# The row transform of the next image at the end of this image's program

## The reference

```
f      = fftshift(fft2(x))                        per image and channel
amp    = |f|;  gate = sigmoid(amp w_h + b_h) + sigmoid(amp w_l + b_l)
s      = real(ifft2(ifftshift(f * gate)))         the phase is kept
y      = silu(conv3x3(s, w_f) + b_f) + x
z      = layernorm(y) * gamma + beta              over channels

u      = layernorm(z);  y = mamba2(u)             512 rows, each a sequence of 128
z      = z + ff(y);     out = z + fc2(gelu(fc1(layernorm(z))))
```

## Time and profile before

| | |
|---|---|
| median of 3 runs | 4281.23 us (4280.12 to 4282.1) |
| the profiled execution | 4282.0 us, its span 4280.1 us |
| busy, share of the span | PE 93%, DVE 82%, ACT 75%, POOL 60% |
| span of the four images | about 1700 us, some 415 to 440 us each |
| mean granted clock of TensorE | 0.974 of full |

### The profile page before, as it was taken

One profiled execution on the slowest core, in us unless ns is written; L12 is line 12 of the kernel. 1 busy time (PEld: TensorE's weight loads), 2 busy tenths in 40 slices (PEclk: granted clock), 3 DMA queues, 4 the chain that ended last, 5 costly groups with the idle time before them and its releaser, 6 DMA issues.

```text
span 4280.1 us, 95150 instructions
## 1 busy us (share of the span) xinstructions
PE 3983.8 (93%) x31687; PEld 2863.5 (67%) x31687; DVE 3492.5 (82%) x8772; ACT 3194.4 (75%) x4968; POOL 2587.1 (60%) x2713
## 2 busy tenths in 40 slices
PE   7998898799979985799999999999999999999998
PEld 4787578757865885466666666666666666666665
DVE  4568447745775485699999999999999999999997
ACT  4445534553456354699999999999999999999997
POOL 0036103600460056588888888888888888888886
PEclk9999999999989998899999999999999999999999
DMA  2013101400140022111111111111111111111110
GB/s 91 1 53 129 57 2 63 156 20 11 63 164 3 11 72 81 38 41 38 42 39 42 39 42 39 42 39 42 39 39 40 39 42 39 42 39 42 39 42 26
DMA packets 214865, 205.93 MB, mean 48 GB/s; under 512 B 14368, under 2 KB 149152, under 8 KB 214688
## 3 DMA queue, kind: packets, MB, share of 16 engines
q1 hardware_dynamic: 214688, 203.60, 14.6%
HBM read 136.45 MB, written 67.11 MB: 48 GB/s over the span
## 4 chain that ended last, share of the span: by engine, by line
PE 58%; ACT 0%; DVE 0%; POOL 0%; issue 0%; POOLq 0%; DVEq 0%; ACTq 0%
PE g_ps L1043 7%; PE g_ps L1028 6%; PE g_ps L986 6%; PE g_ps L972 5%; PE g_ps L1031 5%; PE g_ps L1060 5%; PE g_ps L1003 3%; PE g_ps L1073 3%; PE g_ps L1079 3%; PE g_ps L1052 3%; PE g_ps L1012 3%; PE g_ps L977 3%; PE g_ps L992 2%; PE g_ps L1068 2%; PE g_ps L965 2%; PE g_ps L997 1%
## 5 line engine op out<-in xcount | busy, mean ns | idle before, releaser
L1355 DVE TENSOR_TENSOR g_mmat<-g_emat,g_ps 128x1024 f32<-128x1024 f32 x512 | 598.9, 1210 | 1.4 <-PE g_ps L1003 1.4
L1194 ACT ACTIVATE g_emat<-g_ps 128x1024 f32<-128x1024 f32 x512 | 521.1, 1024 | 85.7 <-PE g_ps L1031 84.2
L1298 DVE SCALAR_TENSOR_TENSOR g_acc<-g_ps,g_conv_w,g_acc 128x504 f32<-128x504 f32 (+1 forms) x768 | 554.5, 722 | 10.3 <-ACT g_acc L1157 9.9
L873 POOL TENSOR_TENSOR g_acc<-g_acc,g_tap 128x508 f32<-128x508 f32 x384 | 482.5, 1271 | 123.6 <-DVE g_acc L1298 123.6
L613 POOL MEMSET f_s_hi<- 128x192 f32 x4 | 1.0, 258 | 820.7 <-PE f_ps L344 820.7
L1043 PEld LDWEIGHTS g_ps<-g_mmat,g_dtx 128*32 128x32 f32 x8192 | 192.6, 109 | 310.6 <-issue 181.7
L1028 PE MATMUL g_ps<-g_rz,g_l 128*128 128x512 f32 x1024 | 390.0, 462 | 1.6 <-DVE g_z L1383 1.6
L229 PE MATMUL f_ps<-f_s_hi,f_wf_hi 128*128 128x256 f32 x1152 | 360.3, 313 | 5.0 <-DVE f_s_lo L466 5.0
L415 ACT ACTIVATE f_s_hi<-f_ps 128x384 fp32r<-128x384 f32 x256 | 125.7, 491 | 274.0 <-PE f_ps L217 268.9
L1043 PE MATMUL g_ps<-g_mmat,g_dtx 128*32 128x128 f32 x8192 | 329.2, 279 | 0.0
L230 PE MATMUL f_ps<-f_s_lo,f_wf_hi 128*128 128x256 f32 x1152 | 326.2, 283 | 0.0
(11 more groups left out here) (194 smaller groups left out, 12374.3 us busy)
## 6 DMA issues: line engine op xcount, KB each, us to landing
f_xt<-in_x_cols SPq DMA_DIRECT2D x32, 1024.0 KB, 10.3
f_xres<-in_x SPq DMA_DIRECT2D x128, 256.0 KB, 2.8
z<-f_zout SPq DMA_DIRECT2D x128, 256.0 KB, 2.0
g_zin<-z SPq DMA_DIRECT2D x128, 256.0 KB, 2.7
g_zres<-z SPq DMA_DIRECT2D x128, 256.0 KB, 2.9
out<-g_outb SPq DMA_DIRECT2D x128, 256.0 KB, 3.0
f_wf_raw<-in_w_f SPq DMA_DIRECT2D x1, 576.0 KB, 6.9
g_wx<-in_in_proj_t SPq DMA_DIRECT2D x1, 192.0 KB, 2.3
```

The costliest lines, as they stand in the source:

```text
L873: pool.tensor_tensor(acc[:, j, :, 1:], acc[:, j, :, 1:], tap1[:, j, :, 0:P - 1], ALU.add).then_inc(add_p[j], 1)
L1194: act.activation(emat[:, g, :].rearrange("p (b n) -> p b n", b=2), ps[:, D_BANK[g]:D_BANK[g] + 2, :], ACT.Exp).then_inc(e_a[g], 1)
L1298: dve.scalar_tensor_tensor(out=acc[:, j, :, k:], in0=four(ps[:, bank, :])[:, :, 0:P - k], scalar=conv_w[:, j, 3 - k:4 - k], in1=acc[:, j, ...
L1355: dve.tensor_tensor(mmat[:, g, :].rearrange("p (h n) -> p h n", h=HEADS), emat[:, g, :].rearrange("p (h n) -> p h n", h=HEADS), ps[:, CB, ...
```

## The change

The row transform of image b + 1 becomes the last part of image b's program on PE; that of image 0 stands ahead of the loop. The loop over images runs three times, and the last image is written out after it. On ACT and DVE the loop over the eight tiles becomes `row_copy(b, t)`, written out, and its calls for the next image stand among the last steps of this image's convolution:

- ACT: copies 0 and 1 after `center(13, .)`, then `center(14, 0)`, copy 2, `center(14, 1)`, copy 3, `center(15, 0)`, copy 4, `center(15, 1)`, copies 5, 6 and 7.
- DVE: `residual(15, 0)`, `residual(15, 1)`, copy 0, `moments(15, 0)`, copy 1, `moments(15, 1)`, copies 2 to 7. Before, each `moments` followed its `residual`.

The programs of POOL and SP are unchanged.

```diff
 PE
-            with pe.Fori(0, IMAGES) as b:
-
+            def row_transform(b):
                 for t in range(8):
                     pe.wait_ge(x_in[t], b * 16 + 16)
...
+
+            def image(b, last):
                 for j in range(4):
                     pe.wait_ge(y_free[j], b * 8 + 9)
...
                 for k in range(BATCHES - 2, BATCHES):
                     for h in range(2):
                         turn(b, k, h)
+                if not last:
+                    row_transform(b + 1)
+
+            row_transform(0)
+            with pe.Fori(0, IMAGES - 1) as b:
+                image(b, False)
+            image(IMAGES - 1, True)
 ACT
-            with act.Fori(0, IMAGES) as b:
-                with act.Fori(0, 8) as t:
-                    for j in (0, 2):
-                        act.wait_ge(y_mm[j], b * 8 + t + 2)
-                        act.activation(rowspec[:, :, ds(t * 16 + 4 * j, 4)].rearrange("p k c -> p c k"),
-                                       ps[:, 3 + j, :].rearrange("p (c k) -> p c k", c=4), ACT.Copy).then_inc(y_free[j], 1)
+            def row_copy(b, t):
+                for j in (0, 2):
+                    act.wait_ge(y_mm[j], b * 8 + (t + 2))
+                    act.activation(rowspec[:, :, 16 * t + 4 * j:16 * t + 4 * j + 4].rearrange("p k c -> p c k"),
+                                   ps[:, 3 + j, :].rearrange("p (c k) -> p c k", c=4), ACT.Copy).then_inc(y_free[j], 1)
+
+            def image(b, last):
...
                         if n in (1, 2) and k >= 3:
                             center(k - 3, n - 1)
+                            if k > BATCHES and not last:
+                                row_copy(b + 1, 2 * (k - BATCHES) + n - 1)
+                    if k == BATCHES and not last:
+                        row_copy(b + 1, 0)
+                        row_copy(b + 1, 1)
                     if k < BATCHES:
                         middle(k)
+                if not last:
+                    for t in (6, 7):
+                        row_copy(b + 1, t)
+
+            for t in range(8):
+                row_copy(0, t)
+            with act.Fori(0, IMAGES - 1) as b:
+                image(b, False)
+            image(IMAGES - 1, True)
 DVE (row_copy as on ACT, with j = 1 and 3 and tensor_copy)
-                for k in range(BATCHES + 2):
+                for k in range(BATCHES + 1):
...
+                residual(b, BATCHES - 1, 0)
+                residual(b, BATCHES - 1, 1)
+                if not last:
+                    row_copy(b + 1, 0)
+                moments(b, BATCHES - 1, 0)
+                if not last:
+                    row_copy(b + 1, 1)
+                moments(b, BATCHES - 1, 1)
+                if not last:
+                    for t in range(2, 8):
+                        row_copy(b + 1, t)
+
+            for t in range(8):
+                row_copy(0, t)
+            with dve.Fori(0, IMAGES - 1) as b:
+                image(b, False)
+            image(IMAGES - 1, True)
```

More of the change, by code:

```diff
@@ L531, in _, with row_copy, image @@
                 dve.sem_inc(one)
[L532 to L537, removed]
+            def row_copy(b, t):
+                for j in (1, 3):
+                    dve.wait_ge(y_mm[j], b * 8 + (t + 2))
+                    dve.tensor_copy(rowspec[:, :, 16 * t + 4 * j:16 * t + 4 * j + 4].rearrange("p k c -> p c k"),
+                                    ps[:, 3 + j, :].rearrange("p (c k) -> p c k", c=4)).then_inc(y_free[j], 1)
+            def image(b, last):
                 for j in range(4):
```

## The result

The changed kernel takes 4248.3 us (median of 4 runs, 4247.5 to 4250.0) against 4280.7 us for the kernel before on the same chip: a ratio of 0.9924, with a 95% interval of 0.9911 to 0.9938.

A forecast was written before the change was run, and what follows sets the result against it. PE is busiest, so the change counts where PE stands still, in the three seams between images. Seams -27.9, jumps +5.4 and clock +4.2 sum to -18.3 us: 4263 us forecast, range 4251 to 4273.

The forecast's parts named there:

- The woven ladder: Seam between images: early tile 0 and woven copies bring the column transform 31.5 us after `residual(15, 1)`, gaining 27.9 us.
- the third case: Rival: PE's clock also falls at the stop before tile 5, leaving 11.7 us gained, 4269.5 us; chance 0.17.
- An uncovered jump costs between about 3 and 5.8; I take 4.7: PE's jump back between tile 7 and column transform: 2.7 us exposed after cover, 5.4 us lost over two jumps.
- the covered jump: Rival: PE's jump back is covered and the clock holds, so all 27.9 us stay, 4253 us; chance 0.18.
- The 4.7 us of the jump lies near the long end: I take it as fallen: Column transform after each jump starts at half clock rate, losing 2.1 us a jump, 4.2 in all.
- costed at nothing: ACT's 32 table loads of 1.28 us in the copy loop: removing them gains nothing, hidden by ACT's 0.43 us idle a tile.
- without a gap either way: First image's row transform: PE runs on with or without the table loads, so no time changes there.
- The second block: Its copy is passed through once, no cost; rival that its loop refetches code: 246 us, 4509 us, chance 0.04.
- the z stores: Late store after `affine(15, 1)` lands before DVE asks for it near 470, so it costs nothing.
- the fixed load of group 31: DVE's wait before `residual(15, 1)` is this load, landing 8.3 us after issue; taken as unchanged.

The follow-up runs named there:

- traffic: Changed kernel plus six 1 MB memory-to-memory transfers on SP's queue after the last store of each of the first three images: 4259.6 us, ratio 0.9939.
- no jump: Changed kernel with its four images written out on PE, ACT and DVE, so no engine jumps back between images: 4241.6 us, ratio 0.9906.
- loads first: Changed kernel with SP issuing the residual's last four row-group loads ahead of the eight x tiles instead of between them: 4239.5 us, ratio 0.9896.
- unwoven: Changed kernel with all of ACT's and DVE's copies behind the last center and the last moments: 4270.8 us, ratio 0.9973.
- copy-4: Changed kernel with ACT's copy 4 ahead of `center(15, 0)` instead of behind it: 4239.5 us, ratio 0.9897.
- the first experiment: Kernel before with only ACT's eight row copies written out in their old place: 4277.0 us, ratio 0.9989.

## Why the prediction was wrong, point by point

- **The woven ladder: right, a little short.** Forecast, counted from `residual(15, 1)`: PE's stop at 15.6 us, tile 5 at 18.3, PE's end at 29.5, column transform at 31.5 without a jump. Measured in the first seam: 15.4, 17.6, 28.6, and 30.3 in the third seam, which has no jump. Part of the difference is a slip in the sum: `affine(14, 1)` after 446.9 (2.6 us) and `root(15)` (2.4) give 451.9 and not 452.3, so that by its own terms the stop was 2.35 us instead of 2.75, 0.4 a seam; 2.23 was measured. The copies behind the row transform cover 1.76 us and not 1.96. The mechanism is shown from both sides: without the weaving 21 us are lost, and the center named as what holds tile 5 is what holds it. One size was off in the second seam: there tile 5 ran at the low clock behind the 2.2-us stop (12.6 us for the three tiles instead of 11.0), the third case's mechanism, but in one seam of three. It is not rare: of the twelve seams of the four kernels that keep this stop (the changed one, traffic, no jump, loads first) the clock fell there in four. The prediction took the clock as held although its own rows have a fall 2.3 us after a stop, less than its 2.75.
- **"An uncovered jump costs between about 3 and 5.8; I take 4.7": the step that failed most.** Behind the row transform PE stood 2.35 and 2.28 us, against 1.76 where no jump is: 0.6 and 0.5 us exposed, 1.1 in all instead of 5.4. All three rows of PE's jump from which 4.7 was taken lie where x tiles were moving (a DMA share of 1.05 to 1.07 in the stretches shown with the traffic kernel). With six copies put behind the image the jump cost 6.92 - 1.76 = 5.2 and 6.21 - 1.76 = 4.5 us beyond the 1.76. That the jump is code being fetched, as the prediction read it, is borne out by the instruction packet at each jump. So the price follows what else is queued, which the prediction had as a rival (the covered jump, 0.18), with the right evidence, the empty queues, and weighed too low. The Trainium skill ("Runtime: NRT & Kernel Launch", Instruction fetch mechanics) says that a taken branch to a block of code that is not held forces a fetch before work goes on; the traces agree, with the packet and the stop, and add that the stop here went from 2.3 to 6.2 and 6.9 us with the traffic.
- **"The 4.7 us of the jump lies near the long end: I take it as fallen": failed with it.** After stops of 2.35 and 2.28 us the clock fell once in two; that once cost 1.7 us (the column transform's first group at 1.98 instead of 1.12 us a pair), and as much was gained in image 0 by luck, as said under the table. Over the two jumps each of the unwoven, the copy-4 and the loads-first kernels it fell once in six, in the copy-4 kernel. With the 6 to 7 us stops of the traffic kernel it fell both times.
- **Table loads "costed at nothing": failed.** The idle 0.43 us a tile was taken as slack, but the chain that sets the tile's pitch ran through the load: without it the pitch fell from 3.66 to 3.57 us, and ACT now idles 0.73 us ahead of each copy. It cost 0.09 us a tile.
- **The convolution: not in the sum at all.** The change says nothing about it, yet the stretches from the convolution to the last residual gained 2.9 us over four images. Shifting DVE's code by eight instructions alone removes the same twenty stalls. That they went in the changed kernel because its code lies elsewhere is the reading; shown is that position suffices to move them. That the stalls also make the 1.5 us of the second stretch is not shown: it ends with the wait for a load.
- **The first image "without a gap either way":** 0.8 us less. Some 0.5 to 0.7 of it can be the table loads, 0.09 us a tile by the first experiment; but the start of that column transform lay between 57.9 and 59.6 us over the ten traces, in kernels without the loads too, so it stays open.
- **The second block, the z stores, the fixed load of group 31:** as forecast; no instruction packet moves in the loop of the second block (none between 1835 and 4160 us), and the load landed 8.5 us after its issue.

Added up: of the 15.3 us between forecast and trace, the jump is 4.3 and its clock 4.1, the ladder 2.0, the two stretches that are put down to the code's position 2.9, the first image 0.8, and 1.2 is the spread of the second block. The jump's 4.3 is a price mis-sized; of the clock's 4.1, 1.6 is luck.

## To carry to other kernels

Price a stall where it will happen, not where it was seen: a jump read off beside a megabyte of traffic says little about one on quiet queues, and when the trace itself offers a reason for a cheaper case (here the DMA share), the forecast should be made for that case. Idle time on an engine inside a tight exchange is not slack until the exchange is walked through once: what waits for whom, and does the load stand in that circle. And when an edit changes the time more than its trace does at the place edited, look for the clock and for stretches that no edit touched before crediting the edit; the kernel without jumps gained 8.7 us by the mark, of which less than half was its own.

## What the runs showed of the hardware that was not expected

- DVE lost 0.36 to 0.38 us once an image at one instruction and 0.16 to 0.20 us four times at another, with no releaser, in both traces where its program lay as before, in every image, and at neither place after a shift by eight instructions, which left one of 0.19 us an image elsewhere. The Trainium skill ("Runtime: NRT & Kernel Launch", Instruction fetch mechanics) calls the cost of crossing from one block of code to the next mostly hidden; if that is what these stalls are, and the instruction packets behind them speak for it, it was not wholly hidden here. No run shows which boundary it is.
- A taken jump on PE: about 0.5 us beyond the work that covered it on quiet queues, 4.5 to 5.2 us with six 1 MB transfers queued. On quiet queues PE's code packet started about 1 us before PE's last matmul ended, under traffic 2.8 to 3.5 us after it.
- The clock's fall at the start of the gates, to 0.50 for 3 to 7 us, came in 38 of 40 images of the ten traces and missed two of one kernel with no edit nearby; an image that it misses is about 2.4 us shorter. Differences of 2 us an image between two kernels can be this alone.
